# A selective scan in 64 steps: which product with C runs on GpSimd, when TensorE spreads C, and two PSUM fills moved from TensorE to ScalarE

## The reference, cut to what matters

```python
h = jax.nn.relu(adj @ x @ gcn_w + gcn_b)
h = (h - mu) * lax.rsqrt(var + EPS) * ln_g + ln_b
xz = h @ w_in;  xc, z = xz[:, :256], xz[:, 256:]
u = jax.nn.silu(causal_conv4(xc) + conv_b)
dbc = u @ w_xp                               # 8 columns for dt, 16 for B, 16 for C
dt = jax.nn.softplus(dbc[:, :8] @ w_dt + b_dt)
dA = jnp.exp(dt[:, :, None] * A[None])       # 256 channels x 16 states
dBu = dt[:, :, None] * B[:, None, :] * u[:, :, None]
def step(hst, inp):
    hst = dAt * hst + dBut
    return (hst, hst @ Ct)
y = ys + u * D_skip
out = (y * jax.nn.silu(z)) @ w_out
```

## Time and profile before

| what | us |
|---|---|
| median of 3 runs | 918.31 |
| fastest and slowest run | 918.03, 923.39 |
| profiled execution, its own time | 922.9 |
| its span, first to last instruction | 921.1 |
| PE, DVE, ACT, POOL busy | 812.2, 684.2, 516.1, 235.3 |
| mean granted clock of PE | 0.936 |

### The profile page before, as it was taken

How to read it: one execution, slowest core, us unless ns; L and a number is a source line. 1 busy time by engine, 2 the same in 40 slices (tenths; PEclk the granted TensorE clock), 3 DMA queues, 4 the chain that set the end, 5 groups by cost and what they waited for, 6 DMA issues and landing times. The chain is left out here.

```text
span 921.1 us, 11988 instructions
## 1 busy us (share of the span) xinstructions
PE 812.2 (88%) x4192; PEld 522.0 (57%) x4192; DVE 684.2 (74%) x976; ACT 516.1 (56%) x838; POOL 235.3 (26%) x135
## 2 busy tenths in 40 slices
PE   6999989999999999999589979989969889796664
PEld 6655538888888888864345559974322233331211
DVE  3986989999999999517752337863177889889997
ACT  2753537777777787535320127532566667766561
POOL 2000000000000000000020010001399879868992
PEclk8999998999999999999889989999879989897767
DMA  8689885220122021059300000000332615606310
GB/s 282 223 307 339 343 293 224 92 92 22 69 91 91 0 91 46 1 213 422 124 1 1 1 1 1 1 1 23 73 102 71 138 47 130 136 26 155 86 46 11
DMA packets 38958, 101.64 MB, mean 110 GB/s; under 512 B 6113, under 2 KB 11114, under 8 KB 32386
## 3 DMA queue, kind: packets, MB, share of 16 engines
q1 hardware_dynamic: 38354, 100.83, 33.1%
q10 hardware_dynamic: 560, 0.27, 0.1%
HBM read 75.60 MB, written 18.14 MB: 102 GB/s over the span
## 5 line engine op out<-in xcount | busy, mean ns | idle before, releaser
L1789 PE MATMUL PS<-big 128*128 128x256 f32 x768 | 194.6, 385 | 3.4 <-ACT big L1619 3.2
L221 PE MATMUL PS<-ident,big 128*128 128x128 f32 x1123 | 159.1, 282 | 41.2 <-ACT big L656 19.2
L221 PEld LDWEIGHTS PS<-ident,big 128*128 128x128 f32 x1123 | 137.6, 146 | 64.0 <-issue 39.3
L463 POOL TENSOR_TENSOR big<-big 128x1024 f32<-128x1024 f32 x64 | 149.6, 2354 | 14.0 <-DVE big L1359 9.4
L1789 PEld LDWEIGHTS PS<-big 128*128 128x128 f32 x768 | 133.7, 191 | 21.7 <-ACT big L1619 7.0
L1619 ACT ACTIVATE big<-PS 128x512 f32<-128x512 f32 x192 | 105.0, 598 | 58.8 <-PE PS L221 57.9
L1359 DVE TENSOR_TENSOR_SCAN big<-PS,stripes,big 128x512 f32<-128x512 f32 x96 | 116.6, 1263 | 4.7 <-ACT PS L722 2.4
L414 POOL MEMSET big<- 128x16 f32 x1 | 0.1, 125 | 462.6 <-DVE big L1168 462.6
L1988 DVE SCALAR_TENSOR_TENSOR big<-big,rz 128x2048 f32<-128x2048 f32 x48 | 112.7, 2350 | 0.9
L1966 DVE CUSTOM_DVE_ANT_0 big<-big 128x2048 f32<-128x2048 bf16 x48 | 109.7, 2289 | 0.1
L722 ACT ACTIVATE PS<-big,stripes 128x512 f32<-128x512 f32 x128 | 85.9, 685 | 34.5 <-DVE big L1359 34.1
(11 more groups left out here) (210 smaller groups left out, 1006.0 us busy)
## 6 DMA issues: line engine op xcount, KB each, us to landing
big<-in_adj SPq DMA_DIRECT2D x16, 2048.0 KB, 8.9
big<-at_dram SPq DMA_DIRECT2D x4, 4096.0 KB, 27.1
at_dram<-big SPq DMA_DIRECT2D x3, 4096.0 KB, 16.5
big<-b_dram SPq DMA_DIRECT2D x32, 256.0 KB, 4.3
big<-big SPq DMA_DIRECT2D x24, 256.0 KB, 4.0
big<-b_dram SPq DMA_DIRECT2D x36, 128.0 KB, 3.9
at_dram<-big SPq DMA_DIRECT2D x1, 3072.0 KB, 18.4
big<-e_dram SPq DMA_DIRECT2D x3, 1024.0 KB, 6.8
```

Source lines behind the costliest of these rows:

```text
L221: return nc.tensor.transpose(PS[:, bank, col:col + P], src, ident[:])
L463: nc.gpsimd.tensor_tensor(dbu[k % 3], du2[c % 2][:, 2 * (n % 2):2 * (n % 2) + 2, :], bb[group % 2][:, pair_of(k) % 2, :].unsqueeze(1).to_b ...
L1789: m = nc.tensor.matmul(PS[:, 4 + k // 3, 0:256], hw[:, jt, h, :], qt[v % 4][:, 256 * c:256 * c + 256], start=(h == 0 and jt == 0), stop=(h ...
```

## The change

`POOLS` becomes (1, 4, 6). With it step 62, which the limit `k < STEPS - 3` keeps off POOL, falls to DVE, so POOL has 23 products and DVE 41, in place of 24 and 40. Spreads are needed at steps 0, 2, 5 and 7 of every eight in place of 2, 5 and 6. Each spread is issued right ahead of the sum of DVE's last product before it, and the first one ahead of the loop. The term u * D_skip is written to PSUM by ACT (`skip`) for the chunks 1 to 3, after `y_done`; the bias of the graph convolution likewise for the chunks 1 to 3, in `a_copy`, from rows that one more DMA loads. On PE the transposes of h for chunks 2 and 3 move from n = 1 to n = 2, behind the output product.

```diff
--- before.py
+++ after.py
@@ -262,7 +262,7 @@
         dg = wt[:, 13:15, :]
         STEPS = STATES * NCH
         Z_STEP = [13] * (NCH - 1) + [6]
-        POOLS = (0, 1, 4)
+        POOLS = (1, 4, 6)
 
         def on_pool(k):
 
@@ -293,6 +293,13 @@
         def spreads_to(k):
 
             return sum(spreads(i) for i in range(k + 1))
+
+        def spread_after(k):
+
+            if on_pool(k):
+                return None
+            own = [i for i in range(k + 1, STEPS) if not on_pool(i)]
+            return own[0] if own and spreads(own[0]) else None
 
         def sums_with(k):
 
@@ -347,6 +354,9 @@
                 sp.dma_start(twice[96:96 + DTR], t["L3_gnn_w_dt"].rearrange("k (q r) -> k q r", r=HALF)).then_inc(w4_in, 16)
                 sp.dma_start(twice[96 + DTR:97 + DTR],
                              t["L3_gnn_b_dt"].rearrange("(o q r) -> o q r", o=1, r=HALF)).then_inc(w4_in, 16)
+            sp.wait_ge(l2_xev, 4)
+            sp.wait_ge(w3_in, 16 * 10)
+            sp.dma_start(dgt[:], t["L3_gnn_gcn_b"].partition_broadcast(P)).then_inc(w3_in, 16)
             sp.wait_ge(x_ready, 12)
             sp.dma_start(cwb, t["L3_gnn_conv_w"].partition_broadcast(P)).then_inc(cw_in, 16)
 
@@ -595,6 +605,11 @@
                 if c:
                     act.wait_ge(ht_mm, c)
                 act_copy(ahg, PS[:, bank, :]).then_inc(a_ev, 1)
+                if c:
+                    act.wait_ge(a_ev, 2 * c)
+                    act.wait_ge(w3_in, 16 * 11)
+                    act_copy(PS[:, bank, :].rearrange("p (s f) -> p s f", f=P),
+                             dgt[:].unsqueeze(1).to_broadcast([P, 4, P])).then_inc(a_ev, 1)
 
             def relu(c, bank):
 
@@ -721,6 +736,13 @@
                     act.wait_ge(scan_done, j - 2)
                 nc.scalar.activation(PS[:, 5 + j % 3, :], dt2[c % 2][:, q, :], ACT.Exp,
                                      scale=na[:, q, pair_of(k):pair_of(k) + 1]).then_inc(da_ready, 1)
+
+            def skip(c):
+
+                act.wait_ge(y_done, c)
+                for b in range(DI):
+                    m = act_copy(PS[:, 2 + b, :], u[:, b, :], scale=dskip[:, b:b + 1])
+                m.then_inc(skip_mm, 1)
 
             def save_state(k):
 
@@ -783,6 +805,8 @@
                         decay(j)
                 if c < NCH - 1:
                     save_state(k)
+                if c and n == 0:
+                    skip(c)
                 if c < NCH - 2:
                     chunk_after(c + 2, n)
                 if c < NCH - 1:
@@ -960,11 +984,13 @@
 
             def gcn(c, bank):
 
-                pe.wait_ge(a_ev, c + 1)
-                nc.tensor.matmul(PS[:, bank, :], ones_row, gcn_b.unsqueeze(1).to_broadcast([1, 4, P]), start=True, stop=False)
+                pe.wait_ge(a_ev, 2 * c + 1)
+                if c == 0:
+                    nc.tensor.matmul(PS[:, bank, :], ones_row, gcn_b.unsqueeze(1).to_broadcast([1, 4, P]), start=True,
+                                     stop=False)
                 for s in range(4):
                     m = nc.tensor.matmul(PS[:, bank, s * P:(s + 1) * P], ahg[:, s * P:(s + 1) * P], gcn_w, start=False,
-                                         stop=(s == 3))
+                                         stop=(c > 0 or s == 3), skip_group_check=(c > 0))
                 m.then_inc(g_mm, 1)
 
             def h_fill(c, bank):
@@ -1036,12 +1062,13 @@
                 c, n = k // STATES, k % STATES
                 if n == 0:
                     if c:
-                        pe.wait_ge(y_done, c)
+                        pe.wait_ge(skip_mm, c + 1)
                     else:
                         pe.wait_ge(dt_ready, dt_count(0, 3))
-                    for b in range(DI):
-                        m = nc.tensor.matmul(PS[:, 2 + b, :], dg[:, b, :], u[:, b, :], start=True, stop=False, skip_group_check=True)
-                    m.then_inc(skip_mm, 1)
+                        for b in range(DI):
+                            m = nc.tensor.matmul(PS[:, 2 + b, :], dg[:, b, :], u[:, b, :], start=True, stop=False,
+                                                 skip_group_check=True)
+                        m.then_inc(skip_mm, 1)
                 if on_pool(k):
                     pe.wait_ge(hcp_ready, pool_before(k + 1))
                     v = hcp[pool_before(k) % 2]
@@ -1082,11 +1109,11 @@
 
             def next_chunk(c, n):
 
-                if n == 1:
+                if n == (1 if c == 1 else 2):
                     if c >= 2:
                         pe.wait_ge(zg_ready, 3 * (c - 1))
                     h_fill(c, 0)
-                elif n == 2:
+                if n == 2:
                     conv_part(c, 0, 0, range(0, 2))
                 elif n == 3:
                     conv_part(c, 0, 0, range(2, 4))
@@ -1131,19 +1158,20 @@
                 elif n == 13:
                     gcn(c, 1)
 
+            spread(next(k for k in range(STEPS) if spreads(k)))
             for k in range(STEPS):
                 c, n = k // STATES, k % STATES
-                if spreads(k):
-                    spread(k)
-                if n == 1 and 0 < c < NCH - 1:
-                    next_chunk(c + 1, n)
                 for i in sums_at(k):
+                    after = spread_after(i)
+                    if after is not None:
+                        spread(after)
                     add_up(i)
-                if c < NCH - 1 and (n != 1 or c == 0):
-                    next_chunk(c + 1, n)
                 if c and n == 1:
                     pe.wait_ge(yg_ready, c)
+                    pe.wait_ge(h_ready, c + 2 if c < NCH - 1 else c + 1)
                     out_product(c - 1, 1, range(4), o_mm)
+                if c < NCH - 1:
+                    next_chunk(c + 1, n)
                 this_chunk(c, n)
                 if c < NCH - 2:
                     chunk_after(c + 2, n)
```

## The result

The changed kernel is slower: ratio 1.0065 to the kernel before, 95% interval 1.0039 to 1.0090, from 20 runs each. The medians are 927.73 us (919.73 to 931.79) and 920.35 us (917.32 to 929.26); the ratio goes with the means, 927.3 and 921.4 us, and not with the medians, which lie 0.8% apart. The profiled execution took 931.15 us with a span of 929.3, 8.2 us more than before.

What follows compares the result with a forecast made beforehand. PE, full in chunks 0 and 1, was taken to bound the kernel through a loop of PE's run and a chain of short work. Terms summed to -1.4 us, with +1.2 for the clock -0.2: 918.0 us, 8-in-10 range 910.5 to 927.

Steps and rivals of the forecast that it cites:

- PE's run in chunk 0: PE from transposes of h to second z product: skip product, spread and sum move into the hole; -2.8 us.
- the chain, twice: Short work from second z product to next transposes of h, 8.7 to 12.7 us: +4.0 each for chunks 1 and 2.
- PE's run in chunk 1: PE from transposes to second z product: skip, bias, a sum and waits leave, two waits come; -3.4 us.
- chunk 2 to the second softplus: 34.3 us to 31.2: removed spread waits partly count, against a new DVE stall at step 39; -3.1 us.
- the second softplus to the gate: Second softplus to `y_done` of chunk 3: POOL's product of step 46 comes between its inputs; 26.4 against 25.6, +0.8 us.
- chunk 3: DVE waits 0.75 us at the start, 1.6 of its 2.02 us hole go, tail after step 60 same; -0.9 us.
- the clock, forecast apart: Longer hole starts PE's run colder: +0.6 us for each of two output products, +1.2 us.
- the first rival: Cold starts: half clock lasts beyond the output product through the convolution in each of three runs; 927.5 us, chance 0.20.
- The stall of step 39: In chunk 2, DVE waits about 2.9 us for a decay behind two silus of u and a table load.
- DVE's 15.7 us were on the path: Rival: with PE relieved, DVE's 15.7 us of waits go and only new stalls stay; 910 us, chance 0.18.
- the new spreads come late and decide: Rival: spreads still stand behind PE's chunk work; steps 40 and 47 come 2.5 us late each; 923 us, chance 0.12.

Runs made afterwards that it cites:

- e4: Changed kernel with ACT's skip term of chunks 1 and 2 behind `h_scale`, and PE's output product ahead of the chunk's first sum: 1.0006 of the kernel before.
- e8: Kernel before, POOLS still (0, 1, 4), with only the early spreads added: 1.0006 of the kernel before.
- e2: Kernel before with POOLS = (1, 4, 6) and nothing else changed: 1.0032 of the kernel before.
- e10: Kernel before with five unused f32 matmuls on PE in the hole ahead of the transposes of h, chunks 1 and 2: 0.9942 of the kernel before.
- e7: Changed kernel with six unused f32 matmuls on PE in each of the two holes ahead of the output product: 1.0012 of the kernel before.
- e5: e4 with POOLS back at (0, 1, 4): 0.9979 of the kernel before.
- e12: e5 with graph convolution bias on PE, four unused matmuls in the holes of chunks 1 and 2, one at each of the last seven steps: 0.9907 of before.
- e11: Changed kernel with DVE's gate product and `y_done` ahead of its product of steps 16, 32 and 48: 1.0050 of the kernel before.

## Why the prediction was wrong

I forecast no change, -0.2 us; it is +6 us by the ratio. The terms of the sum, each against what the two traces show, counted from the last of the first chunk's softplus steps (the sum is made before rounding):

| term | forecast | measured |
|---|---|---|
| PE's run in chunk 0 | -2.8 | -1.8 |
| the chain, twice | +8.0 | +8.0 |
| PE's run in chunk 1 | -3.4 | 0.0 |
| chunk 2 to the second softplus | -3.1 | -1.3 |
| the second softplus to the gate | +0.8 | +0.5 |
| chunk 3 | -0.9 | +1.5 |
| the clock, forecast apart | +1.2 | in the rows above |
| sum | -0.2 | +7.1 |

So the cost of the change was found, and the gains that were to pay for it were not there. The median of the changed kernel, 927.73 us, is next to the 927.5 of the first rival, which I gave 0.20, but that is luck: the median before was 920.35 in the same measurement and not the 918.31 that both sums start from, the loss is 6 us and not 9.5, and the rival's half clock through the convolution is not in the trace (1.99 us at 748.29, full clock).

**The chain between the runs: right.** 12.7 us predicted, 12.65 measured at both boundaries; DVE waits 1.87 us for the decay of step 18 (2.3 said). e4 shows that this is where the loss can be undone.

**PE's run in chunk 1, -3.4: this step failed.** It is 54.81 us after and 54.78 before. The parts that I took away went, and the two waits that I added came (0.87 for `ht_copy`, 0.96 at n = 8). Missing were 0.91 us before dt at 765.78, where ACT's copy of dt, B and C now stands behind two decays and the norm of the chunk before, with no sum on PE in between to hide it; 1.0 and 0.7 us for the graph convolution at 766.83 and the sum at 769.71, where the clock is at half again; and 0.1 more on the output product than the 0.6 that I priced. That is 2.7 of the 2.8 us that the step and its clock term were short.

**PE's run in chunk 0, -2.8.** The second z product ends 62.0 us after the last of the first chunk's softplus steps, 63.8 before: -1.8. The rest is again the clock in the middle of the run, four records in 3.26 us at 705.71 where 1.98 is usual.

**The clock, +1.2: the term was in the wrong place.** I priced it at the two output products, 0.6 each. There it added 0.7 and 0.1 (3.75 us each after, 3.01 and 3.62 before). What it added besides, 1.7 us in chunk 1 and 1.3 or more in chunk 0, stands in the middle of the runs, where I had put nothing. I had also read the earlier trace rows wrongly: 0.75 over the 5 us from 740 means 2.5 us at half, so the clock is back at about 742.5, 3.1 us after the transposes begin and not 1. The output product at 3.01 us was cold for most of its time; with the hole filled it takes 1.95. The Trainium skill says ("TensorE: Matmul & The Clock Gate", section "HAM oscillation") that a pause between short bursts throttles PE again and the next burst starts at half rate, there for waits on DMA, here on other engines; the output product at 3.75 us behind the hole and 2.02 with it filled agrees.

The half clock behind the holes is a cost of both kernels, not of the change: filling gains 4.9 us in the changed kernel and 5.3 in the one before by the ratios, and the two filled kernels (1.0012 and 0.9942) lie 0.0070 apart, the two unfilled 0.0065. The fall in the middle of the run, which the fillings did not remove, is only read from traces; its cause stays open.

**Chunk 2 to the second softplus, -3.1.** Measured 33.15 against 34.41 us: -1.3. The stall of step 39 came as predicted (2.58 us, 2.9 said). What I left out is the same wait of PE for ACT's copy, here 2.63 us. PE's timeline of the changed kernel in chunk 2:

```profile
833.31 1.12 PE L1035 MATMUL PS<-big,wt 9*128 9x512 f32 x2 [2.63 <-ACT big L333]
```

**The second softplus to the gate, +0.8.** Measured 25.8 against 25.3: +0.5, with the scan of step 49 waiting 1.04 us for POOL as said.

**Chunk 3, -0.9.** Measured 53.3 against 51.8: +1.5. The wait of 2.02 us for the decay behind `z_out` is gone, and the one at the start is 0.41 (0.75 said). But DVE waits 1.68 us for the spread of step 56, one of the eight new ones, behind a z product at half clock, and at the end 2.65 us for the last sums, where I had called the tail the same. DVE's timeline of the changed kernel in chunk 3:

```profile
871.15 3.63 DVE L1387 TENSOR_TENSOR_SCAN big<-PS,stripes,big 128x512 f32<-128x512 f32 x3 [0.41 <-ACT PS L737]
...
897.46 1.23 DVE L1398 TENSOR_TENSOR big<-PS,big 128x1024 f32<-128x1024 f32 x1 [1.68 <-issue]
...
921.09 1.29 DVE L1403 TENSOR_TENSOR big<-PS,big 128x512 f32<-128x512 f32 x2 [2.65 <-PE PS L1079]
```

Before, that last wait was 1.18 us, with 0.55 more ahead of the last product. Every kernel with the early spreads has 1.81 (e8) to 2.65 us in that place, e2 and e10 without them have 1.18. The 1.68 is not in e7, whose chunk 3 has the same instructions and takes 51.0 us; so this stretch differs by 2 us between traces, and its +1.5 is the least certain row of the table.

**The rivals.** That DVE's 15.7 us were on the path is refuted by e8. That the new spreads come late and decide is not borne out for chunk 1: DVE waits 2.58 us at step 24, and PE feels 0.96 of it before 773.76, which I had priced at 0.9. At step 56 it is true for 1.68 us, in this trace. The POOL placement alone costs 0.0032 (e2), which I had not listed as a cost of its own; in the later versions taking it back gave 0.0027 (e4 to e5, intervals that overlap). Why it lengthens PE's run by 2.2 us in e2 was seen only in part, as later spreads and sums, and stays open.

## What to carry to other kernels

Before costing an edit by the waits that it removes, find which engine's run closes the loop: here 14 us of DVE's waits vanished (e8) and came back as waits for another engine, because PE was full and ACT's queue stood between. When work moves to a less busy engine, look at what is queued behind it there; a term that must wait for a late signal belongs behind everything that the next stage needs. And price a hole on PE twice, as the time in it and as the half-rate work that follows, about 2 us behind each hole of the changed kernel. Ask then whether the kernel before pays that already, because only the difference belongs to the change. Filling the holes with unused matmuls was the cheapest gain of this study, 0.6% in the kernel before; the best version (e12), with the holes and the last chunk filled and the order mended, is 0.9% faster than the kernel before.

## What was unexpected of the hardware

Unused f32 matmuls at the start of chunks 1 and 2, mostly in idle time of PE (5.7 us of them in each chunk in e7, 4.56 in e10), made the kernel faster by about 5 us, twice (e7, e10). The granted clock over 729 to 747 us was 0.81 before, 0.72 in the changed kernel, 0.66 in e11 and 1.00 in e7. A shorter chain does not help where the clock returns later: e11 took 1.15 us out of the chain and got 1.8 us more in the run. And the clock fell in the middle of a run of the changed kernel, shortly after 765.78, when PE had waited 0.87 us at its start and 0.91 us just before; in the kernel before, with one wait of 1.37 us and one of 0.82, it did not fall in that run.
